# LoRA kernel: the last two groups of sequences split their down product in one 128x64 piece, and share out the last four additions anew

## The reference

```
B_sel = B[adapter_ids]                       # [64, 16, 1024]
A_sel = A[adapter_ids]                       # [64, 1024, 16]
Bx  = einsum('bni,bri->bnr', x, B_sel)       # "down": 1024 -> 16
out = einsum('bnr,bor->bno', Bx, A_sel)      # "up": 16 -> 1024
return x + out * 1.0
```

## Time and profile before

| | us |
|---|---|
| median of 3 runs (91.74 to 92.14) | 92.03 |
| profiled execution | 92.17 |
| its span, first to last instruction | 90.4 |
| PE busy | 81.4 |
| DVE, ACT busy | 59.7, 59.5 |
| last store issued (from the start of the span) | 84.8 |
| mean traffic of the DMA engines | 385 GB/s |

### The profile page before, as it was taken

One profiled execution on the slowest core, in us unless ns is written; L12 is line 12 of the kernel. 1 busy time (PEld: TensorE's weight loads), 2 busy tenths in 40 slices (PEclk: granted clock), 3 DMA queues, 4 the chain that ended last, 5 costly groups with the idle time before them and its releaser, 6 DMA issues.

```text
span 90.4 us, 3583 instructions
## 1 busy us (share of the span) xinstructions
PE 81.4 (90%) x1451; PEld 61.7 (68%) x1451; DVE 59.7 (66%) x111; ACT 59.5 (66%) x154; POOL 62.9 (70%) x141
## 2 busy tenths in 40 slices
PE   3998999989999999999999999999999999989200
PEld 3997778748786878787878787786868687443000
DVE  0309968276595868777686959595959595999000
ACT  1339869939696969696969695968687776542200
POOL 6103992999999998979696979797969792800000
PEclk9999999999999999999999999999999999999955
DMA  1999999999999999999999999999999999997980
GB/s 27 315 401 419 415 406 415 401 413 406 406 410 410 402 424 413 406 419 417 413 421 413 422 413 410 415 422 406 421 417 413 421 410 397 406 383 314 408 335 24
DMA packets 9297, 34.82 MB, mean 385 GB/s; under 512 B 450, under 2 KB 962, under 8 KB 9282
## 3 DMA queue, kind: packets, MB, share of 16 engines
q1 hardware_dynamic: 7552, 27.79, 76.8%
q10 hardware_dynamic: 1730, 6.82, 18.6%
HBM read 17.83 MB, written 16.78 MB: 383 GB/s over the span
## 4 chain that ended last, share of the span: by engine, by line
PE 82%; DMA 6%; ACT 4%; issue 1%
PE t_bank L255 35%; PE bx_bank L268 21%; PE y_banks L288 18%; DMA x_all<-in_A 6%; PE y_banks L315 2%; PE t_bank L319 2%; ACT x_all L365 1%; PE bx_bank L319 1%; ACT b_table L369 1%; PE y_banks L242 1%; PE bx_bank L315 1%; ACT x_all L424 1%; ACT x_t L377 1%; PE t_bank L315 1%; PE bx_bank L242 0%
## 5 line engine op out<-in xcount | busy, mean ns | idle before, releaser
L465 DVE TENSOR_TENSOR x_all<-y_banks,x_all 128x1024 f32<-128x1024 f32 x29 | 35.5, 1225 | 15.4 <-PE y_banks L288 15.0
L377 ACT COPY x_t<-t_bank 128x512 f32<-128x512 f32 x64 | 34.4, 591 | 13.6 <-PE t_bank L255 12.8
L198 POOL CAST a_duo<-a_table 128x512 fp32r x64 | 36.6, 613 | 3.5 <-PE y_banks L288 1.8
L255 PE MATMUL t_bank<-ident,x_all 128*128 128x128 f32 x256 | 35.0, 280 | 0.4 <-ACT x_t L377 0.4
L255 PEld LDWEIGHTS t_bank<-ident,x_all 128*128 128x128 f32 x256 | 27.4, 141 | 7.4 <-issue 5.2
L188 POOL COPY b_duo<-b_table 128x256 f32 x64 | 22.8, 399 | 6.0 <-PE bx_bank L268 6.0
L268 PE MATMUL bx_bank<-x_t,b_duo 128*32 128x64 f32 x1024 | 20.8, 222 | 0.0
L268 PEld LDWEIGHTS bx_bank<-x_t,b_duo 128*32 128x32 f32 x1024 | 15.8, 109 | 5.4 <-issue 5.4
L288 PE MATMUL y_banks<-a_duo,bx_parts 64*128 64x512 f32 x112 | 17.3, 420 | 0.3 <-issue 0.3
L456 DVE TENSOR_TENSOR bx_parts<-bx_bank,bx_parts 32x64 fp32r<-32x64 f32 x64 | 14.1, 220 | 1.4 <-ACT bx_parts L392 0.3
L392 ACT CAST bx_parts<-bx_bank 32x64 fp32r<-32x64 f32 x64 | 13.0, 204 | 1.9 <-PE bx_bank L268 1.3
(11 more groups left out here) (31 smaller groups left out, 22.2 us busy)
## 6 DMA issues: line engine op xcount, KB each, us to landing
x_all<-in_x SPq DMA_DIRECT2D x5, 2048.0 KB, 28.6
out_y<-x_all ACTq DMA_DIRECT2D x3, 2048.0 KB, 15.4
x_all<-in_x SPq DMA_DIRECT2D x4, 1024.0 KB, 14.0
out_y<-x_all SPq DMA_DIRECT2D x1, 3072.0 KB, 14.0
out_y<-x_all SPq DMA_DIRECT2D x6, 512.0 KB, 4.7
x_all<-in_x SPq DMA_DIRECT2D x4, 512.0 KB, 7.2
out_y<-x_all SPq DMA_DIRECT2D x1, 2048.0 KB, 9.7
out_y<-x_all SPq DMA_DIRECT2D x2, 1024.0 KB, 6.7
```

Source lines behind the costliest of these rows:

```text
L198: last = nc.gpsimd.tensor_copy(a_duo[duo % 2][:, k, :], a_table[:, bass.ds(adapters[k] * BANK, BANK)])
L255: last = nc.tensor.transpose(t_bank[unit % 2][:, c * P:(c + 1) * P], x_all[:, 2 * duo + tile, at:at + P], ident[:, :])
L377: nc.scalar.copy(x_t[duo % 2][:, half * HALF:(half + 1) * HALF, tile, :], t_bank[unit % 2][:, :].rearrange("p (c n) -> p c n", c=HALF)).th ...
L465: nc.vector.tensor_tensor(here, product, here, ALU.add).then_inc(y_drained, 1)
```

## The change

For duos 14 and 15 (`FLAT`) the split works on all 128 partitions at once. ScalarE copies the bank to a new buffer `high_flat` (one 128x64 operation), VectorE subtracts that and writes `rest_flat` (one 128x64 operation), and ScalarE moves both to their places in `bx_parts`: four 32x64 copies of the high part, and four more, new on this engine, of the rest (`copy_rest`). It then doubles them at once, ahead of the next duo's split. ScalarE waits for its own semaphore after the first copy and before the doubling.

VectorE now takes both additions of duo 13 in a row, and adds tiles 28, 29 and 31 in whole. Tile 30 is the one that TensorE and ScalarE do, in `t_bank`. The two `x_into` stand between the up products of duo 14. `y_drained` now counts tiles 28, 29 and 31 as 29, 30 and 31, and SyncE waits for these and, for tile 30, for `sum_copied`.

```diff
@@ -33,6 +33,7 @@
     WARM_UPS = 21
+    FLAT = (DUOS - 2, DUOS - 1)
     SQUARE = 2 * RANK
@@ -64,6 +65,8 @@
         ident = sb("ident", [P, P])
+        high_flat = sb("high_flat", [P, 2, SEQ], F32R)
+        rest_flat = sb("rest_flat", [P, 2, SEQ], F32R)
         twice = sb("twice", [P, P], F32R)
@@ -103,6 +106,9 @@
         rest_done = sem("rest_done")
         parts_done = sem("parts_done")
@@ -148,14 +154,12 @@
             for first, end in STORES:
-                if end <= TILES - 3:
+                if end <= TILES - 2:
                     sp.wait_ge(y_drained, end)
-                elif end == TILES - 2:
+                elif end == TILES - 1:
                     sp.wait_ge(sum_copied, HALVES)
                 else:
-                    sp.wait_ge(y_drained, first)
-                if end == TILES:
-                    sp.wait_ge(sum_copied, HALVES + 1)
+                    sp.wait_ge(y_drained, TILES - 1)
                 sp.dma_start(out_rows[:, first:end, :], x_all[:, first:end, :]).then_inc(stored, 16)
@@ -315,48 +319,53 @@
 
-            def x_into(bank, tile, h):
-                nc.tensor.matmul(bank, ident[:, :], x_all[:, tile, :][:, h * BANK:(h + 1) * BANK],
+            def x_into(h):
+                nc.tensor.matmul(t_bank[h][:, :], ident[:, :], x_all[:, TILES - 2, :][:, h * BANK:(h + 1) * BANK],
                                  start=True, stop=False)
 
+            def last_up(duo, tile, bank):
+                for s in range(PER_TILE):
+                    for h in range(HALVES):
+                        last = product(bank[:, h * BANK:(h + 1) * BANK], duo, tile * PER_TILE + s, h,
+                                       s == 0, s == PER_TILE - 1)
+                last.then_inc(y_filled, 1)
+
             before, end = DUOS - 2, DUOS - 1
-            for h in range(HALVES):
-                x_into(t_bank[h][:, :], TILES - 3, h)
             pe.wait_ge(a_gathered, before + 1)
...
             pe.wait_ge(y_drained, 2 * before - 1)
+            last_up(before, 0, y_banks[0])
+            x_into(0)
+            pe.wait_ge(y_drained, 2 * before)
+            last_up(before, 1, y_banks[1])
+            x_into(1)
+            pe.wait_ge(a_gathered, end + 1)
+            pe.wait_ge(parts_done, end + 1)
             for s in range(PER_TILE):
                 for h in range(HALVES):
-                    last = product(y_banks[0][:, h * BANK:(h + 1) * BANK], before, s, h, s == 0, s == PER_TILE - 1)
-            last.then_inc(y_filled, 1)
-            for s in range(PER_TILE):
-                for h in range(HALVES):
-                    last = product(t_bank[h][:, :], before, PER_TILE + s, h, False, s == PER_TILE - 1)
+                    last = product(t_bank[h][:, :], end, s, h, False, s == PER_TILE - 1)
             last.then_inc(sum_filled, 1)
-
-            pe.wait_ge(a_gathered, end + 1)
-            pe.wait_ge(parts_done, end + 1)
-            pe.wait_ge(y_drained, 2 * before)
-            for s in range(PER_TILE):
-                for h in range(HALVES):
-                    last = product(y_banks[1][:, h * BANK:(h + 1) * BANK], end, s, h, s == 0, s == PER_TILE - 1)
-            last.then_inc(y_filled, 1)
             pe.wait_ge(y_drained, 2 * before + 1)
-            for s in range(PER_TILE):
-                last = product(y_banks[0][:, 0:BANK], end, PER_TILE + s, 0, s == 0, s == PER_TILE - 1)
-            last.then_inc(y_filled, 1)
-            x_into(bx_bank[before % 2][:, :], TILES - 1, 1)
-            for s in range(PER_TILE):
-                last = product(bx_bank[before % 2][:, :], end, PER_TILE + s, 1, False, s == PER_TILE - 1)
-            last.then_inc(sum_filled, 1)
+            last_up(end, 1, y_banks[0])
 
...
 
+            def copy_rest(duo):
+                act.wait_ge(flat_rest_done, FLAT.index(duo) + 1)
+                for k in range(DUO_SEQS):
+                    s = k % PER_TILE
+                    last = nc.scalar.copy(bx_parts[duo % 2][QUAD:K_UP, k, s * SEQ:(s + 1) * SEQ],
+                                          rest_flat[k * QUAD:(k + 1) * QUAD, duo % 2, :])
+                last.then_inc(rest_copied, 1)
+
             def double_parts(duo):
-                act.wait_ge(rest_done, duo + 1)
+                if duo in FLAT:
+                    act.wait_ge(rest_copied, FLAT.index(duo) + 1)
+                else:
+                    act.wait_ge(rest_done, duo + 1 - sum(d < duo for d in FLAT))
                 nc.scalar.copy(own_tokens(duo, K_UP, 2 * K_UP),
@@ -383,6 +392,11 @@
                 act.wait_ge(bx_done, duo + 1)
+                if duo in FLAT:
+                    if duo - 2 in FLAT:
+                        act.wait_ge(flat_rest_done, FLAT.index(duo - 2) + 1)
+                    nc.scalar.copy(high_flat[:, duo % 2, :], bx_bank[duo % 2][:, 0:SEQ]).then_inc(flat_high_done, 1)
+                    act.wait_ge(flat_high_done, FLAT.index(duo) + 1)
                 if duo < 2:
@@ -390,7 +404,8 @@
                     last = nc.scalar.copy(bx_parts[duo % 2][0:QUAD, k, s * SEQ:(s + 1) * SEQ],
-                                          bx_bank[duo % 2][k * QUAD:(k + 1) * QUAD, 0:SEQ])
+                                          high_flat[k * QUAD:(k + 1) * QUAD, duo % 2, :] if duo in FLAT
+                                          else bx_bank[duo % 2][k * QUAD:(k + 1) * QUAD, 0:SEQ])
                 last.then_inc(high_done, 1)
@@ -406,23 +421,19 @@
                     copy_a(A_BY_ACT[1])
-                if duo == DUOS - 1:
-                    split_high(duo)
-                if duo:
+                if duo and duo - 1 not in FLAT:
                     double_parts(duo - 1)
...
                     copy_x(duo + 1, 3)
-                if duo + 1 < DUOS:
-                    split_high(duo)
-            double_parts(DUOS - 1)
+                split_high(duo)
+                if duo in FLAT:
+                    copy_rest(duo)
+                    double_parts(duo)
             act.wait_ge(sum_filled, 1)
             for h in range(HALVES):
-                nc.scalar.copy(x_all[:, TILES - 3, :][:, h * BANK:(h + 1) * BANK],
+                nc.scalar.copy(x_all[:, TILES - 2, :][:, h * BANK:(h + 1) * BANK],
                                t_bank[h][:, :]).then_inc(sum_copied, 1)
-            act.wait_ge(sum_filled, 2)
-            nc.scalar.copy(x_all[:, TILES - 1, :][:, BANK:D],
-                           bx_bank[(DUOS - 2) % 2][:, :]).then_inc(sum_copied, 1)
 
@@ -449,6 +460,13 @@
             def split_rest(duo):
+                if duo in FLAT:
+                    dve.wait_ge(flat_high_done, FLAT.index(duo) + 1)
+                    if duo - 2 in FLAT:
+                        dve.wait_ge(rest_copied, FLAT.index(duo - 2) + 1)
+                    nc.vector.tensor_tensor(rest_flat[:, duo % 2, :], bx_bank[duo % 2][:, 0:SEQ],
+                                            high_flat[:, duo % 2, :], ALU.subtract).then_inc(flat_rest_done, 1)
+                    return
                 dve.wait_ge(high_done, duo + 1)
@@ -465,19 +483,20 @@
             split_rest(0)
-            for duo in range(1, DUOS - 1):
+            for duo in range(1, DUOS - 2):
                 add_x(duo - 1, 0)
...
                 add_x(duo - 1, 1)
+            split_rest(DUOS - 2)
+            add_x(DUOS - 3, 0)
+            add_x(DUOS - 3, 1)
             split_rest(DUOS - 1)
             add_x(DUOS - 2, 0)
-            dve.wait_ge(y_filled, TILES - 2)
-            here = x_all[:, TILES - 2, :]
-            product = y_banks[1][:, :]
+            add_x(DUOS - 2, 1)
+            dve.wait_ge(y_filled, TILES - 1)
+            here = x_all[:, TILES - 1, :]
+            product = y_banks[0][:, :]
             nc.vector.tensor_tensor(here, product, here, ALU.add).then_inc(y_drained, 1)
-            dve.wait_ge(y_filled, TILES - 1)
-            first_half = x_all[:, TILES - 1, :][:, 0:BANK]
-            nc.vector.tensor_tensor(first_half, y_banks[0][:, 0:BANK], first_half, ALU.add).then_inc(y_drained, 1)
 
```

More of the change, by code:

```diff
@@ L105, in lora_kernel @@
         rest_done = sem("rest_done")
+        flat_high_done = sem("flat_high_done")
+        flat_rest_done = sem("flat_rest_done")
+        rest_copied = sem("rest_copied")
         parts_done = sem("parts_done")
```

## The result

The changed kernel takes 92.31 us (median of 11 runs, 91.95 to 92.43), the kernel before 92.03 (11 runs): ratio 1.0029, 95% interval 1.0018 to 1.0041. That is 0.28 us more: under the 0.5% that I had called no difference, and yet clear of the noise of so many runs. The profiled execution took 92.29 us (92.17 before), its span 90.3 (90.4 before). So the span is as it was, and what grew is the time outside of it, from 1.8 to 2.0 us.

What follows compares the result with a forecast made beforehand. One DMA engine, behind the others, was taken to bound the kernel. Span 90.4 + change 0 + outside 1.8 gave 92.17 us, that execution being 0.14 above the median: forecast 92.0, own range 91.7 to 92.4, 8-in-10 range 91.0 to 92.5.

Steps and rivals of the forecast that it cites:

- what bounds the kernel: End of the stores: one DMA engine, 1.9 us behind, sets the time; earlier stores are worth nothing to it.
- The point up to which a delay is free: Last store: early enough for the last DMA engine if issued by 87.4 us; forecast issue 83.95.
- The span forecast: Whole span: stays at 90.4 us, a change of 0.
- the working of the change: Splits of duos 14 and 15: SBUF copies 0.25 us each, duo 14's doubling done at 78.0 instead of 78.74.
- the times forecast: Store issue: tile 27 at 78.45, 28 at 80.15, 29 about 82.0, 30 at 83.25, 31 at 83.95 us.
- Rival A: Last stores: their issue sets the end, so filled DMA troughs save 0.95 us, giving 91.1 us; chance 0.15.
- Rival C: ScalarE's longer chain delays stores past 87.4 us; could cost some 0.5 us, giving 92.5 us; chance 0.03.
- one term of the sum: Time outside the span: 1.8 us, carried over unchanged from the kernel before.
- Rival B: Behind 75 us: one more instruction fetch on the DMA engine ending last costs 1.05 us, giving 93.1; chance 0.05.

Runs made afterwards that it cites:

- e5: Kernel before, with the last store held back by a GpSimd copy of 128x1536 that SyncE waits for; ratio 1.0005.
- e12: Changed kernel with 25 more semaphore waits on ScalarE at the start, 221 instructions in its program; ratio to the kernel before 1.0013.
- e1: Kernel before with nine more tiny 128x1 copies on ScalarE at the start, 196 instructions in its program; ratio 1.0017.
- e2: Kernel before with four more tiny copies on ScalarE at the start, 191 instructions in its program; ratio 1.0039.
- e13: Kernel before with the store of tiles 12 to 15 cut at row 120 and the first store cut between tiles 15 and 16; ratio 1.0375.

## What the prediction had right, and the step that failed

**Right: what bounds the kernel.** The one engine that is alone at 88.6 to 89.4 is there after the change too, and the landing moved by 0.1 us while tile 28's store moved by 1.24 us, tile 27's by 0.85 and the last by 0.5, and tile 30's came 0.76 us later (83.64 against 82.88). Delays of the last store by 1.07 us (e5) and 1.9 us (e12 against the changed kernel) cost nothing; 3.24 us cost 1.0. The point up to which a delay is free was put at 87.4 and came out at 87.0. The span forecast was 90.4; measured are 90.3 in the profile and 90.25 in the mean, against 90.14 to 90.20 in the mean of the kernel before on three occasions.

**Right: the working of the change.** Copies from SBUF 0.25 us each, and, with the 0.24 us of later start taken off, the doubling of duo 14 ends 0.7 us earlier (78.24 against 78.74). That of duo 15 is no earlier; here it is before and after the change:

```profile
80.36 0.40 ACT L360 CAST bx_parts<-bx_parts 64x256 fp32r<-64x256 f32 x1 [1.61 <-DVE bx_parts L456]
```

```profile
80.58 0.40 ACT L369 CAST bx_parts<-bx_parts 64x256 fp32r<-64x256 f32 x1
```

The stores, less that 0.24, came within 0.15 us of the times forecast. Rival A's filled troughs came, and were worth nothing, as the forecast had it. Rival C's stall didn't come.

**The step that failed: one term of the sum.** "The sum against the profiled execution is 90.4 + 0 + 1.8": the 1.8 us outside of the span were carried over without a reason, as if the change couldn't touch them. Measured are 2.03 against 1.79, so this term was 0.24 us too small. That is nearly all of the 0.28 us by which the kernel got slower, where the forecast was 92.0, no change. What the runs show in its place is a time outside of the span that depends on the length of ScalarE's program: nine small copies more in the kernel before, hidden at the start, raise it from 1.79 to 1.95 (e1). The ratio of e1 alone, 1.0017 with an interval from 0.9999, would not show it. By which mechanism is open, and so is the rest of the 0.24. Rival B had come near it, with the instruction queue and "ScalarE a few more", but it took its price of 1.05 us from the 16 KB packets of q8 and looked for the fetch among the stores. The packets whose number moves with ScalarE's length are the 8 KB ones of q14.

**Open.** Why one engine is behind, and whether it is the same in each execution. How far it is behind is not: in the profiles of e1 and e2 the pack works until about 88.3 and one engine until 89.1, 0.8 us in place of 1.9. Instruction fetches are a candidate, not shown. A version of the kernel that would shorten the last engine's share was tried once (e13) and failed, so none beats the kernel before.

## What to carry to other kernels

When the DMA engines are full to the end, don't read their mean: look at the last microseconds of the windows, find how many engines are still at work, and count back how far behind the last one is. What is issued sooner than that engine can take it is worth nothing. Split a measured difference into span and rest before explaining it: nine instructions more on one engine cost 0.16 us outside of the span here (e1), while all that the change moved inside was worth nothing.

## What the runs showed that I had not expected

- ScalarE's program of 187, 191, 196 and 221 instructions: 1.79, 2.14, 1.95 to 2.03 and 1.84 us outside of the span, and mean spans that agree within 0.2 us.
- A store cut in three, at tile 16 and at row 120 of 128, the same bytes, made the kernel 3.75% slower, with TensorE standing idle for up to 2.7 us and no wait for data.
- In the kernel before, the time fell by 1.9% without ten of 32 tiles' stores, hardly more than without four (1.8%). In both profiles no engine is behind any more, so there the issue of the last stores sets the end. In the changed kernel (2.1% and 1.3%) one engine still ended alone.
